# Expert matmuls moved between the attention products, one PSUM tensor for the output, and expert weights loaded by two queues

## The chip, the cores and the metric

The kernel runs on one Trainium2 chip, on 8 cores at once. Every core runs the same program on its own sequence of 4096 tokens; the cores exchange nothing. The metric is the device time in microseconds of the slowest core. Profiled executions show in addition each core's span, from its first to its last instruction.

## The reference

A token's 1024 features are normalised to `xn`. Two branches read `xn`, and the output is `x + attention(xn) + expert(xn)`:

```python
xn = _layernorm(x, axis=-1)
# attention branch: heads of ONE token attend to each other (16 heads x 64)
q = xn @ Wq + bq
kv = (xn @ Wdown + bdown) @ Wup + bup          # 1024 -> 256 -> 2048
k, v = split(kv.reshape(B, T, 16, 128))
q, k = apply_rope(q), apply_rope(k)            # same rotation for all heads
att = softmax(einsum('bthd,btgd->bthg', q, k) / sqrt(64))
a = einsum('bthg,btgd->bthd', att, v).reshape(B, T, 1024) @ Wout + bout
# expert branch: top 1 of 8 experts
logits = xn @ router_w.T + router_b
w, top1 = max(softmax(logits)), argmax(logits)
f = (xn @ expert_w[top1].T + expert_b[top1]) * w
```

Query and key of one token are rotated by the same angle, so the rotation drops out of their product, and the kernel leaves it out.

## The kernel before, in words

**Tiling.** A core works through its 4096 tokens in 16 tiles of 256 (`for i in range(nt)`). Ahead of the loop stands a phase of some 400 us, in which weights are loaded and cast to bf16, and the eight expert matrices (2 MB each in bf16) are transposed and written to a tensor in HBM, `exscratch`. SBUF has room for only two expert matrices, the two halves of `exbuf`, so that in each tile all eight are read again, 16 MB.

**One tile.** TensorE's order within a tile is: transpose `xn` (L666), router (L677), `q` (L685), the routing mask (L693, L701), the latent (L708), keys and values (L720), then for the two halves w = 0 and 1 of the tile the transposes of the values and the query-key products (L730 to L752), then the two products of attention with the values, slots `av0` (L760, into PSUM tensor `psb`) and `av1` (L772, into `psa`), then the output projection `wout` (L787, with the bias row at L792), then the eight experts (L804, 64 matmuls of 128x256 each), the expert bias (L811), and the transposes back to token order `yT` (L818). Output projection and experts add up in the same PSUM: four of the eight 256-column blocks in `psb`, four in `psa`, one to a bank.

**The experts.** Every expert is computed for all 256 tokens; VectorE first multiplies `xn` by a mask row that is zero for tokens of another expert, which gives `xe` (L389 for experts 0 and 1, L442 for the others; two buffers). `xe` of expert n may be written once expert n-2 is done (semaphore `sxu`). The weights follow the same rule: SyncE waits on `sxu` for expert n-2 and then issues one DMA of 2 MB into that half of `exbuf` (L832 is the helper's line).

**The softmax.** For each half w VectorE adds a mask, takes the maximum, subtracts (L398 to L407), ScalarE exponentiates (L573, L584), VectorE sums, divides (L413 to L424) and transposes the result into `pav` (L433). There is one `pav`: the transpose for w = 1 waits until `av0` has read the one for w = 0. ScalarE then copies each half's product from PSUM to `o_f` (slots `of0`, L597, and `of1`, L608). Of the eight `xe` multiplies the last six stand behind the second transpose in VectorE's list.

**What sets the order.** Nothing reorders instructions. Each engine has its own list, written by hand, and the engines wait for each other by counters: TensorE's, ScalarE's and VectorE's steps have numbered slots (`T_SLOTS`, `S_SLOTS`, `V_SLOTS`), and `tensor.wait_ge(smV, vv(i, 'pav0'))` waits until VectorE has passed slot `pav0` of tile i. L197 and L475 in the profile are the helpers that close such a slot on VectorE and ScalarE. GpSimd's list only issues DMAs in the loop: after the last step of a tile (`yadd`) the load of the tokens two tiles ahead, and the two stores of the output (L170).

Of the kernel before, what the change touches and what calls it, by code (L numbers as in the profile page):

```python
# [17 lines left out]
           'vT0', 'qk0', 'vT1', 'qk1', 'av0', 'av1', 'wout', 'expert', 'yT']  # L18
# [5 lines left out]
P0_T = 4 + 64  # L24
P0_S = 65
P0_V = 53
P0_SEX = 16 * 8
# [14 lines left out]
def build_core(dbg_dump=None, nt=NT, phase0_only=False):  # L42
# [22 lines left out]
    with ExitStack() as st:  # L65
# [72 lines left out]
        sex1 = e(nc.semaphore("sex1"))  # L138
        sexp = e(nc.semaphore("sexp"))
# [14 lines left out]
        def _(gpsimd):  # L154
# [24 lines left out]
            if not phase0_only:  # L179
# [3 lines left out]
                for i in range(nt):  # L183
                    gpsimd.wait_ge(smV, vv(i, 'yadd'))
                    if i + 2 < nt:
                        xload(i + 2)
                    for g in range(2):
                        gdma(out_d[TOK * i + 128 * g:TOK * i + 128 * (g + 1), :],
                             outsb[:, 1024 * g:1024 * (g + 1)], so)

        @block.vector
        def _(vector):
# [92 lines left out]
            for i in range(nt):  # L285
# [161 lines left out]
                vector.wait_ge(smT, tv(i, 'expert'))  # L447
                if i > 0:
                    vector.wait_ge(smT, tv(i - 1, 'yT'))
                srcyb = re(psb[:], "p (m x) -> p m x", x=512)[:, :, 0:256]  # L450
                vector.tensor_copy(out=re(y_f[:, 0:1024], "p (m x) -> p m x", x=256),
                                   in_=srcyb)
                srcya = re(psa[:], "p (m x) -> p m x", x=512)[:, :, 0:256]
                vector.tensor_copy(out=re(y_f[:, 1024:2048], "p (m x) -> p m x", x=256),
                                   in_=srcya)
# [14 lines left out]
        def _(scalar):  # L470
# [22 lines left out]
            for i in range(nt):  # L493
# [95 lines left out]
                for hl in range(2):  # L589
                    for a in range(4):  # L590
                        srco = re(psb[64 * hl:64 * hl + 64, :],
# [21 lines left out]
        def _(tensor):  # L613
# [7 lines left out]
            li = None  # L621
# [38 lines left out]
            for i in range(nt):  # L660
# [95 lines left out]
                tinc(li)  # L756
                tensor.wait_ge(smV, vv(i, 'pav0'))
                for ol in range(16):
                    for a in range(4):
                        li = tensor.matmul(  # L760
                            out=psb[:, 512 * a + 32 * ol:512 * a + 32 * (ol + 1)],
# [5 lines left out]
                tinc(li)  # L767
                tensor.wait_ge(smV, vv(i, 'pav1'))
                tensor.wait_ge(smS, sv(i, 'extr1'))
# [11 lines left out]
                tensor.wait_ge(smS, sv(i, 'of0'))  # L781
                tensor.wait_ge(smS, sv(i, 'of1'))
                def pout(m):
                    return (psb if m < 4 else psa)[:, 512 * (m % 4):512 * (m % 4) + 256]
                for m in range(8):
                    for k in range(8):
# [4 lines left out]
                                      start=(k == 0), stop=False)  # L791
                    li = tensor.matmul(out=pout(m),  # L792
                                       lhsT=bo_r[:, 128 * m:128 * (m + 1)],
                                       rhs=ones_b[:], start=False, stop=False)
                tinc(li)
                for ex in range(8):
                    n = 8 * i + ex
                    tensor.wait_ge(sxv, n + 1)
                    tensor.wait_ge(sex0 if n % 2 == 0 else sex1, 16 * (n // 2 + 1))
                    eb = 8192 * (n % 2)  # L800
                    xb = 2048 * (ex % 2)
                    for m in range(8):
                        for k in range(8):
                            li = tensor.matmul(out=pout(m),  # L804
                                               lhsT=exbuf[:, eb + 1024 * k + 128 * m:
                                                           eb + 1024 * k + 128 * (m + 1)],
                                               rhs=xe[:, xb + 256 * k:xb + 256 * (k + 1)],
                                               start=False, stop=False)
                    li.then_inc(sxu, 1)
                for m in range(8):  # L810
                    li = tensor.matmul(out=pout(m),  # L811
                                       lhsT=exb[:, 128 * m:128 * (m + 1)],
# [134 lines left out]
```

## Time and profile before

| | us |
|---|---|
| Time, median of 3 runs (lowest, highest) | 3315.51 (3314.82, 3319.16) |
| The profiled execution's own time | 3312.88 |
| Its span on the slowest core, core 1 | 3311.3 |
| Spans of the eight cores | 3260.0 to 3311.3 |
| TensorE matmuls busy | 1932.0 (58%) |
| VectorE busy | 861.2 (26%) |
| ScalarE busy | 558.2 (17%) |
| GpSimd busy | 35.0 (1%) |

A page of the profile has the busy time of each engine, the span in 40 slices with TensorE's granted clock (1.00 is 2.4 GHz, 0.50 is 1.2 GHz), the DMA queues, the chain of work that ended last, and the costliest groups of instructions with the idle time before them and what ended it. PE is TensorE, PEld its weight loads, DVE VectorE, ACT ScalarE, POOL GpSimd, SP SyncE. An ending q, as in DVEq, is the engine's sequencer, here nearly always a slot being closed. The DMA queues are two: q1, issued by SyncE, moved 330.40 MB, and q0, issued by GpSimd, 33.56 MB. On the chain that ended last TensorE has 47% of the span, DMA 20%, VectorE 14% and ScalarE 8%.

### The profile page before, as it was taken

Reading aid. Unit: us, or ns where it says so; the run is one execution under the profiler, and the core shown is the slowest. Engines: PE = TensorE matmul, PEld = TensorE weight load, DVE = VectorE, ACT = ScalarE, POOL = GpSimd, SP = SyncE. Lnnn points to the kernel's source line nnn. Section 1 sums busy time; section 2 is a strip of 40 time slices with the busy share of each in tenths; the row PEclk is TensorE's granted clock in tenths of the full one; section 3 lists DMA queues with packets and bytes.
Section 4 is the critical chain, followed back from the end, with each engine's and each line's share of the span. In section 5 each row is a group of like instructions: output and inputs, shape, how many; then the busy total and the mean of one; then the engine's idle time right before and its main releaser. Section 6 shows DMA issues by size and latency. Waiting matters only on the chain.

```text
span 3311.3 us, 38330 instructions; the slowest of 8 cores (3260.0 to 3311.3 us)
## 1 busy us (share of the span) xinstructions
PE 1932.0 (58%) x16558; PEld 1572.4 (47%) x16558; DVE 861.2 (26%) x1041; ACT 558.2 (17%) x770; POOL 35.0 (1%) x74
## 2 busy tenths in 40 slices
PE   0011158576675757485766657574858576575758
PEld 0011147455454636374555546363646455463636
DVE  2111131322323232313223232323131322323231
ACT  0122230211112030303011120303030211203030
POOL 0000000000000000000000000000000000000000
PEclk9855569687776869596867768686969677776869
DMA  5344414132240506050322315060504133140504
GB/s 157 135 152 152 168 61 178 52 131 99 80 150 33 197 1 229 1 200 29 136 94 83 147 45 185 1 229 1 209 20 166 64 115 115 56 174 8 209 1 165
DMA packets 42362, 366.40 MB, mean 111 GB/s; under 512 B 5059, under 2 KB 6083, under 8 KB 24532
## 3 DMA queue, kind: packets, MB, share of 16 engines
q1 hardware_dynamic: 32980, 330.40, 27.2%
q0 software_dynamic: 9216, 33.56, 3.2%
q8 instruction: 132, 2.16, 0.3%
q14 instruction: 34, 0.28, 0.0%
HBM read 330.39 MB, written 33.55 MB: 110 GB/s over the span
## 4 chain that ended last, share of the span: by engine, by line
PE 47%; DMA 20%; DVE 14%; ACT 8%; issue 4%; DVEq 4%; ACTq 3%; SPq 1%; POOL 0%; POOLq 0%
DMA exbuf<-exscratch 13%; PE psb L804 9%; PE psa L804 8%; PE psb L720 6%; DMA y_f<-exw 5%; PE psb L685 5%; PE psa L677 3%; PE psb L787 3%; ACTq L475 3%; DVE pav L433 2%; DVE pdiag L424 2%; PE psa L787 2%; ACT koct L544 2%; ACT vdm L549 2%; DVEq L197 2%
## 5 line engine op out<-in xcount | busy, mean ns | idle before, releaser
L804 PE MATMUL psb<-xe,exbuf 128*128 128x256 bf16 x4096 | 485.6, 279 | 94.7 <-DMA exbuf<-exscratch 94.5
L804 PEld LDWEIGHTS psb<-xe,exbuf 128*128 128x128 bf16 x4096 | 402.8, 100 | 168.8 <-issue 113.3
L804 PE MATMUL psa<-xe,exbuf 128*128 128x256 bf16 x4096 | 468.1, 273 | 0.0
L804 PEld LDWEIGHTS psa<-xe,exbuf 128*128 128x128 bf16 x4096 | 400.8, 98 | 46.4
L442 DVE TENSOR_TENSOR xe<-xnf,mrep 128x2048 bf16<-128x2048 bf16 x96 | 117.6, 1225 | 917.9 <-PE psa L804 917.9
L720 PE MATMUL psb<-lat,wup_sb 128*128 128x256 bf16 x1024 | 190.9, 365 | 123.0 <-ACTq L475 123.0
L496 ACT ACTIVATE lnv<-mv,epsc 128x2 f32<-128x2 f32 x16 | 4.8, 300 | 1334.3 <-DVEq L197 1334.3
L720 PEld LDWEIGHTS psb<-lat,wup_sb 128*128 128x128 bf16 x1024 | 125.9, 127 | 188.4 <-issue 147.9
L651 PE MATMUL psa<-idbf,exbuf 128*128 128x128 bf16 x512 | 49.4, 280 | 260.0 <-DVE exbuf L280 256.7
L651 PEld LDWEIGHTS psa<-idbf,exbuf 128*128 128x128 bf16 x512 | 46.0, 131 | 263.3 <-issue 263.1
L677 PE MATMUL psa<-rT_sb,xnf 128*128 128x8 f32 x512 | 111.5, 361 | 79.1 <-DVEq L197 79.1
L685 PE MATMUL psb<-xnf,wq_sb 128*128 128x256 bf16 x1024 | 152.5, 325 | 0.0
L677 PEld LDWEIGHTS psa<-rT_sb,xnf 128*128 128x128 f32 x512 | 110.4, 332 | 83.7 <-issue 83.7
L666 PE MATMUL psb<-id,xn_t 128*128 128x128 f32 x256 | 56.1, 411 | 149.2 <-ACTq L475 149.2
L685 PEld LDWEIGHTS psb<-xnf,wq_sb 128*128 128x128 bf16 x1024 | 121.3, 120 | 30.1
L787 PE MATMUL psb<-o_f,wo_sb 128*128 128x256 bf16 x512 | 104.9, 373 | 43.0 <-ACTq L475 43.0
L666 PEld LDWEIGHTS psb<-id,xn_t 128*128 128x128 f32 x256 | 51.4, 224 | 153.9 <-issue 153.9
L280 DVE CAST exbuf<-y_f 128x2048 bf16<-128x2048 f32 x32 | 39.3, 1227 | 260.1 <-DMA y_f<-exw 260.1
L487 ACT COPY exbuf<-psa 128x1024 bf16<-128x1024 bf16 x64 | 59.4, 1049 | 250.3 <-PE psa L651 250.3
L367 DVE TENSOR_TENSOR qoct<-qoct,qpatb 128x4096 bf16<-128x4096 bf16 x16 | 36.7, 2292 | 238.2 <-ACTq L475 238.2
L526 ACT ACTIVATE qoct<-psb 64x2048 bf16<-64x2048 f32 x32 | 78.0, 2437 | 121.2 <-PE psb L685 121.1
L772 PE MATMUL psa<-pav,vst 32*128 32x32 bf16 x1024 | 11.0, 187 | 148.6 <-DVEq L197 148.6
(128 smaller groups left out, 1806.1 us busy)
## 6 DMA issues: line engine op xcount, KB each, us to landing
exbuf<-exscratch SPq DMA_DIRECT2D x128, 2048.0 KB, 8.4
y_f<-exw SPq DMA_DIRECT2D x64, 512.0 KB
x_t<-x POOLq DMA_DIRECT2D x32, 512.0 KB, 5.7
exscratch<-exbuf SPq DMA_DIRECT2D x8, 2048.0 KB, 7.8
out<-outsb POOLq DMA_DIRECT2D x32, 512.0 KB, 6.9
y_f<-wq SPq DMA_DIRECT2D x8, 512.0 KB
y_f<-wo SPq DMA_DIRECT2D x8, 512.0 KB
y_f<-wup SPq DMA_DIRECT2D x2, 1024.0 KB
```

The costliest lines, as they stand in the source:

```text
L197: ins = vector.drain()
L424: vector.tensor_tensor(out=dstn, in0=srcn, in1=r3.broadcast_to([32, 16, 32]), op=ALU.mult)
L442: vector.tensor_tensor(out=re(xe[:, 2048 * (ex_i % 2):2048 * (ex_i % 2) + 2048], "p (cc t) -> p cc t", t=256), in0=src0, in1=m1.broadcast_ ...
L475: ins = scalar.drain()
L526: scalar.activation(out=dstq, in_=srcq, func=AF.Identity, scale=0.125)
L651: li = tensor.transpose(out=psa_bf[:, 1024 * (kd % 4) + 128 * jo: 1024 * (kd % 4) + 128 * (jo + 1)], in_=exbuf[:, 1024 * jo + 128 * kd:102 ...
L666: li = tensor.transpose(out=psb[:, 128 * (8 * g + cc):128 * (8 * g + cc + 1)], in_=xn_t[:, 1024 * g + 128 * cc:1024 * g + 128 * (cc + 1)], ...
L677: li = tensor.matmul(out=psa[:, off:off + 8], lhsT=xnf32[:, 128 * (8 * g + cc): 128 * (8 * g + cc + 1)], rhs=rT[:, 8 * cc:8 * cc + 8], sta ...
L685: li = tensor.matmul(out=psb[:, 256 * m:256 * (m + 1)], lhsT=wq[:, 1024 * k + 128 * m: 1024 * k + 128 * (m + 1)], rhs=xnf[:, 256 * k:256 * ...
L720: li = tensor.matmul(out=psb[:, 256 * gch:256 * (gch + 1)], lhsT=wup[:, 4096 * k + 128 * ch: 4096 * k + 128 * (ch + 1)], rhs=lat[:, 256 * ...
L787: tensor.matmul(out=pout(m), lhsT=wo[:, 1024 * k + 128 * m: 1024 * k + 128 * (m + 1)], rhs=o_f[:, 256 * k:256 * (k + 1)], start=(k == 0), ...
L804: li = tensor.matmul(out=pout(m), lhsT=exbuf[:, eb + 1024 * k + 128 * m: eb + 1024 * k + 128 * (m + 1)], rhs=xe[:, xb + 256 * k:xb + 256 * ...
```

## The change

The order within a tile changes on TensorE. After the query-key products come four matmuls that write zeros to all of `psb` (a row of `unit` that holds zeros as the one-row left operand), then experts 0 and 1, then `av0`, experts 2 and 3, `av1`, experts 4 to 7, and last, block by block, the expert bias, the output projection and its bias row. `av0` now writes `psa` as `av1` does, so `av0` waits for `extr1` (ScalarE's copy of the second query-key product out of `psa`), and `av1` for `of0` (ScalarE's copy of `av0`). All eight output blocks stand side by side in `psb`, two to a bank, and VectorE copies them to `y_f` in one instruction. The slots `expert` and `wout` change places.

The load of an expert's weights is split by columns: SyncE issues the first 4096 columns, GpSimd the other 4096, each 1 MB, with the same wait on `sxu` and with semaphores of its own (`sexg0`, `sexg1`), for which TensorE waits too.

```diff
 T_SLOTS = ['xnT', 'router', 'q', 'prepA', 'prepB', 'lat', 'kv0', 'kv1', 'kv2', 'kv3',
-           'vT0', 'qk0', 'vT1', 'qk1', 'av0', 'av1', 'wout', 'expert', 'yT']
+           'vT0', 'qk0', 'vT1', 'qk1', 'av0', 'av1', 'expert', 'wout', 'yT']
...
@@ gpsimd
                 for i in range(nt):
+                    for ex in range(8):
+                        n = 8 * i + ex
+                        if n == 0:
+                            gpsimd.wait_ge(smT, P0_T)
+                            gpsimd.wait_ge(sexp, P0_SEX)
+                        if n >= 2:
+                            gpsimd.wait_ge(sxu, n - 1)
+                        gdma(exbuf[:, 8192 * (n % 2) + 4096:8192 * (n % 2) + 8192],
+                             exs_d[ex][:, 4096:8192],
+                             sexg0 if n % 2 == 0 else sexg1)
                     gpsimd.wait_ge(smV, vv(i, 'yadd'))
...
@@ vector
-                vector.wait_ge(smT, tv(i, 'expert'))
+                vector.wait_ge(smT, tv(i, 'wout'))
                 if i > 0:
                     vector.wait_ge(smT, tv(i - 1, 'yT'))
-                srcyb = re(psb[:], "p (m x) -> p m x", x=512)[:, :, 0:256]
-                vector.tensor_copy(out=re(y_f[:, 0:1024], "p (m x) -> p m x", x=256),
-                                   in_=srcyb)
-                srcya = re(psa[:], "p (m x) -> p m x", x=512)[:, :, 0:256]
-                vector.tensor_copy(out=re(y_f[:, 1024:2048], "p (m x) -> p m x", x=256),
-                                   in_=srcya)
+                vector.tensor_copy(out=y_f[:], in_=psb[:])
+                vector.drain()
                 vinc()
...
@@ scalar, slot of0
-                        srco = re(psb[64 * hl:64 * hl + 64, :],
+                        srco = re(psa[64 * hl:64 * hl + 64, :],
...
@@ tensor
+                def pout(m):
+                    return psb[:, 256 * m:256 * (m + 1)]
+
+                def expert_mms(ex):
+                    n = 8 * i + ex
+                    tensor.wait_ge(sxv, n + 1)
+                    tensor.wait_ge(sex0 if n % 2 == 0 else sex1, 16 * (n // 2 + 1))
+                    tensor.wait_ge(sexg0 if n % 2 == 0 else sexg1, 16 * (n // 2 + 1))
+                    eb = 8192 * (n % 2)
+                    xb = 2048 * (ex % 2)
+                    for m in range(8):
+                        for k in range(8):
+                            li = tensor.matmul(out=pout(m), ..., start=False, stop=False)
+                    li.then_inc(sxu, 1)
+                    return li
+
+                tensor.wait_ge(smS, sv(i, 'kv3ev'))
+                for b in range(4):
+                    tensor.matmul(out=psb[:, 512 * b:512 * (b + 1)],
+                                  lhsT=unit[0:1, 128:256], rhs=unit[0:1, 0:512],
+                                  start=True, stop=False)
+                expert_mms(0)
+                expert_mms(1)
                 tensor.wait_ge(smV, vv(i, 'pav0'))
+                tensor.wait_ge(smS, sv(i, 'extr1'))
                 # av0: 64 matmuls
-                            out=psb[:, 512 * a + 32 * ol:512 * a + 32 * (ol + 1)],
+                            out=psa[:, 512 * a + 32 * ol:512 * a + 32 * (ol + 1)],
                 tinc(li)
+                expert_mms(2)
+                expert_mms(3)
                 tensor.wait_ge(smV, vv(i, 'pav1'))
-                tensor.wait_ge(smS, sv(i, 'extr1'))
+                tensor.wait_ge(smS, sv(i, 'of0'))
                 # av1: 64 matmuls
                 tinc(li)
-                tensor.wait_ge(smS, sv(i, 'of0'))
+                for ex in range(4, 8):
+                    expert_mms(ex)
                 tensor.wait_ge(smS, sv(i, 'of1'))
                 # then, for each of 8 blocks m: exb (1 matmul), wo (8), bo_r (1)
...
@@ sync
-                    dma(exbuf[:, 8192 * (n % 2):8192 * (n % 2) + 8192], exs_d[ex],
+                    dma(exbuf[:, 8192 * (n % 2):8192 * (n % 2) + 4096],
+                        exs_d[ex][:, 0:4096],
                         sem=sex0 if n % 2 == 0 else sex1)
```

How the instructions stand on TensorE before, from the second query-key product to the first experts of a tile (`pav` is the transposed softmax, `vst` the values, `o_f` the attention's output, `wo_sb` its projection, `xe` the masked tokens; `smV`, `smS` are VectorE's and ScalarE's slots):

```order
L752 MATMUL psa<-koct,qoct 128x128 x15
L760 MATMUL psb<-pav,vst 128x32 [waits smV]
L760 MATMUL psb<-pav,vst 128x32 x63
L772 MATMUL psa<-pav,vst 128x32 [waits smV,smS]
L772 MATMUL psa<-pav,vst 128x32 x63
L787 MATMUL psb<-o_f,wo_sb 128x256 [waits smS]
```

And the same place of the changed kernel, up to the fourth expert:

```order
L760 MATMUL psa<-koct,qoct 128x128 x15
L787 MATMUL psb<-unit_sb 128x512 [waits smS]
L787 MATMUL psb<-unit_sb 128x512 x3
L777 MATMUL psb<-xe,exbuf 128x256 [waits sxv,sex0,sexg0]
L777 MATMUL psb<-xe,exbuf 128x256 x63
L777 MATMUL psb<-xe,exbuf 128x256 [waits sxv,sex1,sexg1]
L777 MATMUL psb<-xe,exbuf 128x256 x63
L796 MATMUL psa<-pav,vst 128x32 [waits smV,smS]
L796 MATMUL psa<-pav,vst 128x32 x63
L777 MATMUL psb<-xe,exbuf 128x256 [waits sxv,sex0,sexg0]
L777 MATMUL psb<-xe,exbuf 128x256 x63
```

Two experts now stand between the query-key products and `av0` (L796), two between `av0` and `av1`, and the projection has moved behind the eighth expert.

VectorE's list at the end of the softmax and the start of the later `xe` multiplies is the same in both kernels but for line numbers; this is the changed kernel's:

```order
L425 TENSOR_REDUCE s<-pex 128x16 [waits smS]
L429 RECIPROCAL r<-s 128x16
L436 TENSOR_TENSOR pdiag<-pex,r 32x16x32 x4
L445 STREAM_TRANSPOSE pav<-pdiag 128x2048 [waits smT]
L454 TENSOR_TENSOR xe<-xnf,mrep 128x2048 [waits sxu] x6
L462 COPY y_f<-psb 128x2048 [waits smT]
```

Nothing moved here: the transpose L445 waits for `av0` (through `smT`), and the multiply for expert 2 stands behind it.

GpSimd's list of the changed kernel, from the first tile into the second (each `exbuf` row is half an expert):

```order
L172 DMA exbuf<-exscratch 128x4096 [waits smT,sexp]
L172 DMA exbuf<-exscratch 128x4096
L172 DMA exbuf<-exscratch 128x4096 [waits sxu] x6
L172 DMA x_t<-x 128x1024 [waits smV]
L172 DMA x_t<-x 128x1024
L172 DMA out<-outsb 128x1024 x2
L172 DMA exbuf<-exscratch 128x4096 [waits sxu] x8
```

Before, it held only the `x_t` and `out` rows. The eight expert loads of a tile now stand between one tile's stores and the next tile's token loads.

## Rows read from the trace of the kernel before

**Rows 1.** The page's head, and VectorE's first step of each tile.
```profile
span 3311.3 us, 38330 instructions; the slowest of 8 cores (3260.0 to 3311.3 us)
...
L289 DVE BATCH_NORM_STATS2 stats<-x_t x32: 675/684/695, 401.1 to 3129.4; 128x6 f32<-128x512 f32 x32
```

**Rows 2.** Waits of TensorE, whole run: us in total, times, longest.
```profile
PE psa L772 <- DVEq L197: 148.6, 16, 9.6
...
PE psb L804 <- DMA exbuf<-exscratch: 94.5, 72, 3.5
...
PE psb L760 <- DVEq L197: 88.0, 16, 5.5
...
PE psb L787 <- ACTq L475: 43.0, 16, 2.7
```

**Rows 3.** Timeline of TensorE, one tile: start, length, instructions, idle before.
```profile
844.32 1.87 PE L752 MATMUL psa<-koct,qoct 128*128 128x128 bf16 x16 [2.18 <-ACTq L475]
851.69 0.69 PE L760 MATMUL psb<-pav,vst 32*128 32x32 bf16 x64 [5.50 <-DVEq L197]
861.64 0.69 PE L772 MATMUL psa<-pav,vst 32*128 32x32 bf16 x64 [9.26 <-DVEq L197]
865.01 1.86 PE L787 MATMUL psb<-o_f,wo_sb 128*128 128x256 bf16 x8 [2.69 <-ACTq L475]
866.81 0.39 PE L792 MATMUL psb<-ones_b,bo_row 1*128 1x256 bf16 x1
867.13 1.89 PE L787 MATMUL psb<-o_f,wo_sb 128*128 128x256 bf16 x8
...
873.74 1.05 PE L787 MATMUL psa<-o_f,wo_sb 128*128 128x256 bf16 x8
...
874.93 1.05 PE L787 MATMUL psa<-o_f,wo_sb 128*128 128x256 bf16 x8
...
877.31 3.67 PE L804 MATMUL psb<-xe,exbuf 128*128 128x256 bf16 x32
...
893.67 3.65 PE L804 MATMUL psb<-xe,exbuf 128*128 128x256 bf16 x32 [2.21 <-DMA exbuf<-exscratch]
...
939.84 0.59 PE L811 MATMUL psa<-indw_f,exb_sb 8*128 8x256 bf16 x4
943.14 3.50 PE L818 MATMUL psa<-id,y_f 128*128 128x128 f32 x16 [2.71 <-DVEq L197]
```

**Rows 4.** Groups by line, whole run: busy us, mean ns, idle before.
```profile
L804 PE MATMUL psb<-xe,exbuf 128*128 128x256 bf16 x4096 | 485.6, 279 | 94.7 <-DMA exbuf<-exscratch 94.5
...
L804 PE MATMUL psa<-xe,exbuf 128*128 128x256 bf16 x4096 | 468.1, 273 | 0.0
L442 DVE TENSOR_TENSOR xe<-xnf,mrep 128x2048 bf16<-128x2048 bf16 x96 | 117.6, 1225 | 917.9 <-PE psa L804 917.9
```

**Rows 5.** Groups by line within one tile, 775.44 to 956.12 us.
```profile
L433 DVE STREAM_TRANSPOSE pav<-pdiag 128x2048 bf16<-128x2048 bf16 x2 | 4.6, 2311 | 0.5 <-issue 0.5
...
L308 DVE COPY xnf<-psb 128x2048 f32<-128x2048 f32 x1 | 2.3, 2290 | 7.0 <-PE psb L666 7.0
```

**Rows 6.** Stretches: busy by engine, then TensorE's clock, DMA share, GB/s.
```profile
865.00:871.00 6.00, 5.99 (x26) 3.23 (x26) 0.00 (x0) 0.00 (x0) 0.00 (x0) 0.50 0.01 3
872.00:877.00 5.00, 5.00 (x40) 3.28 (x38) 0.00 (x0) 0.00 (x0) 0.00 (x0) 1.00 0.00 0
...
802.50:803.00 0.50, 0.00 (x0) 0.00 (x0) 0.44 (x1) 0.50 (x1) 0.00 (x0) 0.99 0.00 0
803.00:803.50 0.50, 0.00 (x0) 0.00 (x0) 0.50 (x1) 0.49 (x2) 0.00 (x0) 0.50 0.00 0
```

**Rows 7.** Timeline of TensorE: an expert of the first tile, behind a wait.
```profile
563.90 5.32 PE L804 MATMUL psb<-xe,exbuf 128*128 128x256 bf16 x32 [2.30 <-DMA exbuf<-exscratch]
```

**Rows 8.** DMA issues of the whole run: KB each, median us to landing.
```profile
exbuf<-exscratch SPq DMA_DIRECT2D x128, 2048.0 KB, 8.4
...
x_t<-x POOLq DMA_DIRECT2D x32, 512.0 KB, 5.7
```

**Rows 9.** GpSimd's issues after a tile, and the stretches behind them.
```profile
768.87 1.05 POOL L170 DMA_DIRECT2D x_t<-x  x2 [177.86 <-DVEq L197]
...
769.00:770.00 1.00, 0.00 (x0) 0.00 (x0) 1.00 (x3) 0.00 (x0) 1.00 (x3) 0.50 0.00 0
...
771.00:777.00 6.00, 1.56 (x8) 1.59 (x9) 0.44 (x3) 2.87 (x4) 0.00 (x0) 0.50 0.96 326
```

More of the change, by code:

```diff
@@ L138, in build_core @@
         sex1 = e(nc.semaphore("sex1"))
+        sexg0 = e(nc.semaphore("sexg0"))
+        sexg1 = e(nc.semaphore("sexg1"))
         sexp = e(nc.semaphore("sexp"))
@@ L756, in _ @@
                 tinc(li)
+                def pout(m):
[9 more added lines that the diff above has]
+                        for k in range(8):
+                            li = tensor.matmul(out=pout(m),
+                                               lhsT=exbuf[:, eb + 1024 * k + 128 * m:
+                                                           eb + 1024 * k + 128 * (m + 1)],
+                                               rhs=xe[:, xb + 256 * k:xb + 256 * (k + 1)],
+                                               start=False, stop=False)
+                    li.then_inc(sxu, 1)
[7 more added lines that the diff above has]
+                expert_mms(1)
                 tensor.wait_ge(smV, vv(i, 'pav0'))
+                tensor.wait_ge(smS, sv(i, 'extr1'))
                 for ol in range(16):
@@ L780, in _ @@
                 tinc(li)
-                tensor.wait_ge(smS, sv(i, 'of0'))
+                for ex in range(4, 8):
+                    expert_mms(ex)
                 tensor.wait_ge(smS, sv(i, 'of1'))
-                def pout(m):
-                    return (psb if m < 4 else psa)[:, 512 * (m % 4):512 * (m % 4) + 256]
                 for m in range(8):
+                    li = tensor.matmul(out=pout(m),
+                                       lhsT=exb[:, 128 * m:128 * (m + 1)],
+                                       rhs=indw_f[:], start=False, stop=False)
+                    if m == 0:
+                        tinc(li)
                     for k in range(8):
@@ L790, in _ @@
                                       rhs=o_f[:, 256 * k:256 * (k + 1)],
-                                      start=(k == 0), stop=False)
+                                      start=False, stop=False)
                     li = tensor.matmul(out=pout(m),
                                        lhsT=bo_r[:, 128 * m:128 * (m + 1)],
[L794 to L812, printed above, removed]
-                                       rhs=indw_f[:], start=False, stop=True)
+                                       rhs=ones_b[:], start=False,
+                                       stop=(m % 2 == 1))
                 tinc(li)
```

## The prediction, made before the changed kernel had run

> **What bounds the kernel now.** I read first how often the 16 tiles come round: VectorE's first step of a tile stands at 401.1 us in the first and 3129.4 us in the last, (3129.4 - 401.1) / 15 = 181.9 us apart [rows 1]. The loop is 16 x 181.9 = 2910 of the span's 3311.3 us, so a microsecond saved per tile is 16 in all. Then I read TensorE's waits by what ended them [rows 2], since every engine works through a handwritten list and TensorE's is the longest. Four waits lie in the part of the tile that the change rewrites: 88.0 / 16 = 5.5 us ahead of `av0` and 148.6 / 16 = 9.3 us ahead of `av1` (both for VectorE's softmax), 43.0 / 16 = 2.7 us ahead of the output projection (for ScalarE's copy), and 94.5 / 16 = 5.9 us within the experts, for their weights. Last I read one tile's timeline [rows 3]. TensorE stands in a chain there: query-key product until 846.2, `av0` at 851.69, `av1` at 861.64, projection 865.01 to 877.31, experts from there, bias until 940.4. The experts need only `xe` and weights, which for experts 0 and 1 lie ready, yet they queue behind the whole softmax. So TensorE's order bounds this stretch, with work at hand during 17.5 us of waiting.
>
> **What the change does to each wait.** All terms are per tile, against the profiled execution.
>
> *Waits removed.* Experts 0 and 1 now cover the wait for `pav0`. Two experts run from 877.31 to the next wait at 893.67 - 2.21 = 891.46, 7.1 us each [rows 3]; so 14.2 us of work stand where the wait was 5.5. Before `av1` stand experts 2 and 3, another 14.2 us, and behind it four experts cover ScalarE's copy, 28 us against 2.7. Removed: 5.5 + 9.3 + 2.7 = 17.5 us.
>
> *A wait added.* VectorE has one `pav`. Its second transpose waits for `av0`, and the multiply that makes `xe` for expert 2 stands behind that transpose in VectorE's list. Before, this cost nothing extra since TensorE was itself waiting for the transpose. Now `av0` comes only after experts 0 and 1, the softmax of w = 1 has long been done by then, and VectorE is held at the transpose. From the end of `av0`: 0.25 us for the signal, 2.31 for the transpose [rows 5], 0.25 to the next instruction, 1.23 for the multiply [rows 4], 0.15 to TensorE: 4.2 us in which TensorE idles before expert 2. Queued behind the transpose on VectorE are also the multiplies for experts 3 to 7, but each of those is needed 7 us later than the one before and takes 1.23, so only expert 2 waits. Cost: 4.2 us, and I hold this for certain within 0.5.
>
> *The weights' wait.* A load is issued when expert n-2 ends and lands 8.4 us later in the median [rows 8]; expert n-1 covers 7.1 of it. With 0.2 us for the signals every second expert waits 1.5 us (a wait delays the next issue and so pays for the next expert): 3 x 1.5 = 4.5 by this rule, measured 5.9 [rows 2], a factor of 1.3 for the spread. In the new order expert 2 has 7.1 + 0.9 (`av0` with its signals) + 4.2 = 12.2 us for its load, expert 3 has more than 12, since expert 2 follows the 4.2 us gap, and expert 4 has 7.1 + 0.9 (`av1`). Left are 2 x 1.5 - 0.9 = 2.1, times 1.3 = 2.7 us. Saved: 5.9 - 2.7 = 3.2 us, if both halves of a load together still land in 8.4.
>
> *The two halves.* The trace before has no expert load on GpSimd's queue. The nearest rows are its token loads: issued at 768.87, the share of the DMA engines is 0.00 until 770 and 0.96 after 771, at 326 GB/s [rows 9]. So this queue starts at least 1.1 us after its first issue, and then keeps the engines as full as SyncE's does, which needs 8.4 us for 2 MB. Bounds: the two 1 MB halves overlap their fixed costs and land up to 1 us sooner, or GpSimd's half ends up to 3 us later. A microsecond either way moves the wait by 2 us per tile (experts 4 and 6). I take no change, the value nearest to 8.4, since the bytes and the 16 engines are the same. The Trainium skill says much the same in its page DMA: Bandwidth & Descriptors, section Issuing engines are not separate DMA queues: DMAs of several engines end on the same 16 and gain only the time to start them. [...]
>
> *The clock.* Before, the projection starts at 1.2 GHz (0.50 from 865 to 871) and is at 2.4 GHz from 872 [rows 6]; it takes 877.31 - 865.01 = 12.3 us, and at the high clock a block takes 874.93 - 873.74 = 1.19, eight 9.5. At the tile's end, straight behind four experts, it has the high clock. Saved: 2.8 us. Now expert 0 meets the low clock instead. The clock rose between 871 and 872, some 6.5 us after dense work began at 865.01. Dense work now begins with the query-key product at 844.32 or, at the latest, with expert 0 at about 848.1; so between 2.7 and 6.5 us of expert 0 run at half speed, and half of that is lost, 1.3 to 3.2. I take 1.8, nearer to the first, since TensorE has no wait from 844.32 on. The second place is the new 4.2 us gap with `av0`'s 0.7 us ahead of it. In the trace the clock fell to 0.50 at 803, with TensorE idle [rows 6], and even a wait of 2.30 us was followed by a group of 32 matmuls that took 5.32 instead of 3.65 us, 1.7 lost [rows 3, 7]. So I expect the clock to fall in the gap and expert 2 to start at 1.2 GHz. Bounds 1.7 (that row) and 3.2 (half of 6.5), and 0 if the high clock survives the gap. I take 2.4. On the other side such falls cost the experts 485.6 - 468.1 = 17.5 us in the run [rows 4], 1.1 per tile (some ten falls behind the 72 waits of rows 2), of which with fewer and shorter waits I leave 0.4. Net of the clock: 2.8 + 0.7 - 1.8 - 2.4 = -0.7.
>
> *Small terms.* Four zero matmuls of 512 columns: at the low clock a one-row matmul of 256 columns takes 867.13 - 866.81 = 0.32 us, of which about 0.1 is the change of operands; twice the columns give 0.43 each and 1.9 with the start. At the high clock it would be 1.0. The two signals ahead of `av0` and `av1`, where TensorE now arrives with its partner done: 0.4 in all. The expert bias is moved, 8 matmuls as before: 0. VectorE's one copy of 2048 columns: 2.29 by the like copy from PSUM [rows 5], against the 2.7 us between bias and `yT` that the two copies and their signals take now [rows 3]; one instruction less, one drain more, 0 within 0.1. GpSimd's list: its halves for experts 0 and 1 of the next tile stand behind the token loads and stores issued at about 769; tokens, stores and the two halves are 4 MB, at 326 GB/s 13 us from 770 on, and they are needed at 846, 60 us of cover. The token loads themselves wait for the same slot as before, and six expert loads ahead of them are long issued by then.
>
> **The sum** per tile: 17.5 + 3.2 - 4.2 - 0.7 - 1.9 - 0.4 = 13.5 us saved. Times 16: 216. The profiled execution took 3312.9 us; 3312.9 - 216 = 3097. It stands 2.6 us under the median of the runs, so I forecast 3100 us.
>
> **The rivals.**
> *The clock stays up.* The 4.2 us gap doesn't lower it, and it has risen when expert 0 begins: 2.4 + 1.8 = 4.2 us more per tile, 17.7 in all: 3312.9 - 283 + 2.6 = 3032 us. For it: only some ten of 72 waits in the experts lowered it [rows 2, 4]. Against: the fall at 803 [rows 6]. 12%.
>
> *GpSimd's half is late.* GpSimd's queue moves nothing for 1.1 us after an issue [rows 9], and each of its loads now fires at the moment when VectorE starts an `xe` multiply. With 2 us of lag the wait grows by 4 us per tile: 13.5 - 4 = 9.5, 3164 us. For it: the token loads need 5.7 us for 512 KB [rows 8]. Against: those are 2 MB in flight at once. 20%. The Trainium skill, page SBUF — State Buffer, section Who interferes with whom, has a rule against DMAs issued from GpSimd: while VectorE is in a two-port mode, GpSimd can't write its descriptors; it excepts `tensor_tensor`, as this multiply is. No row before shows such a pair.
>
> *Slower than before.* Two DMAs at once, one on each queue, land later than one of the same bytes, by so much that it eats all. A landing time L beyond 8.4 costs 2 (L - 8.4) at experts 4 to 7, and beyond 12.2 another L - 12.2 at expert 2. The 13.5 us are gone at 3 L = 42.5, L = 14.2 us; at L = 15 the cost is 13.2 + 2.8 = 16.0, and the kernel takes 3315.5 + 16 x 2.5 = 3356 us. It would need 1 MB from GpSimd's queue at some 80 GB/s; rows 9 show 326 for the queue. 3%.
>
> *The change doesn't do what it says.* If weights or `xe` of experts 0 and 1 weren't ready at 846, the wait would only move, and the time be 3310 to 3316. The weights have had since the tile before, and both multiplies stand ahead of the softmax in VectorE's list. 2%. Denser work on all cores could also take the clock in the experts under 1.00; a sixth lost on some 66 us of dense matmuls is 11 us, which leaves 13.5 - 11 = 2.5 and 3276 us. 3%.
>
> **How the numbers follow.** Forecast 60%, 3100, own range 3065 to 3140. With clock kept 12% (3032), late half 20% (3164), slower 3%, no effect 2%, denser work 3%. The range of 8 in 10 reaches from the middle between the forecast and the first rival, 3050, to a little past the late half, 3175. A difference of 0.2% (6.6 us) is about what a measurement of this kernel can tell from none. Faster by more: 60 + 12 + 20 + 3 = 95%; within 2%; slower 3%.
>
> **What would show it.** The period of tiles, 168.4 us instead of 181.9. TensorE's waits ahead of `av0`, `av1` and the projection under 0.5 us each. A wait of about 4.2 us in each tile before expert 2, ended by VectorE's `xe` multiply, and behind it a group at 0.50 clock; if it isn't there, I misread VectorE's list. Waits for expert weights of some 2.7 us per tile, at experts 4 and 6; 6 or more would mean the late half, and then the landing of GpSimd's issues must exceed SyncE's. The projection at 9.5 us plus 0.9 for the bias, all at 1.00. Wrong would be the forecast if the waits vanish as said and the experts themselves take more than 7.1 us.

## The result and the profile after

| | before | changed |
|---|---|---|
| Median, us (lowest, highest; 8 runs each) | 3316.88 (3313.21, 3325.39) | 3104.83 (3100.08, 3116.60) |
| Ratio to before (95% interval) | 1 | 0.9365 (0.9351 to 0.9380) |
| Span of the profiled execution, us | 3311.3 | 3099.9 |

The forecast was 3100 us, in a range of 3050 to 3175. The medians are 212 us apart, 216 were forecast. In some executions of a kernel the cores of one die show a lower granted clock and the time is 1 to 3% longer; the times and ratios below are those of the executions without it.

The page's head and VectorE's first step of each tile answer to [rows 1]:

```profile
span 3099.9 us, 38858 instructions; the slowest of 8 cores (3082.9 to 3099.9 us)
...
L301 DVE BATCH_NORM_STATS2 stats<-x_t x32: 675/682/695, 402.2 to 2922.8; 128x6 f32<-128x512 f32 x32
```

The tiles come (2922.8 - 402.2) / 15 = 168.0 us apart, where the prediction had 168.4, and before 181.9. The first starts at 402, before at 401: all of the gain lies in the loop.

TensorE's waits, as in [rows 2] (us in total, times, longest):

```profile
PE psb L777 <- DVE xe L454: 69.1, 16, 4.5
PE psb L777 <- DMA exbuf<-exscratch: 60.3, 46, 3.1
PE psa L842 <- DVEq L209: 43.3, 16, 3.0
```

No row is left for `av0` (now L796), `av1` (L810) or the projection (L829), which before stood at 88.0, 148.6 and 43.0 us. One row is new: 16 waits of 4.3 us for the `xe` multiply L454. The wait for expert weights fell from 94.5 to 60.3 us.

TensorE's timeline of one tile, which answers to [rows 3] (start, length, instructions, idle before):

```profile
816.09 1.86 PE L760 MATMUL psa<-koct,qoct 128*128 128x128 bf16 x16 [2.18 <-ACTq L483]
817.89 1.88 PE L787 MATMUL psb<-unit_sb 1*128 1x512 bf16 x4
819.70 15.51 PE L777 MATMUL psb<-xe,exbuf 128*128 128x256 bf16 x128
835.15 0.65 PE L796 MATMUL psa<-pav,vst 32*128 32x32 bf16 x64
840.11 15.54 PE L777 MATMUL psb<-xe,exbuf 128*128 128x256 bf16 x128 [4.30 <-DVE xe L454]
855.58 0.65 PE L810 MATMUL psa<-pav,vst 32*128 32x32 bf16 x64
856.52 7.15 PE L777 MATMUL psb<-xe,exbuf 128*128 128x256 bf16 x64 [0.28 <-DMA exbuf<-exscratch]
865.07 14.13 PE L777 MATMUL psb<-xe,exbuf 128*128 128x256 bf16 x128 [1.41 <-DMA exbuf<-exscratch]
880.76 7.15 PE L777 MATMUL psb<-xe,exbuf 128*128 128x256 bf16 x64 [1.56 <-DMA exbuf<-exscratch]
...
901.11 3.57 PE L842 MATMUL psa<-id,y_f 128*128 128x128 f32 x16 [2.69 <-DVEq L209]
```

A row of 128 matmuls is two experts. Behind a wait that left the clock up, or none, two take 14.13 us. The first two of the tile take 15.51 and the next two 15.54, 1.4 us more each: that is the low clock. In other tiles the low clock took more: up to 2.9 us from the first two experts (17.07 us from 1485.53 on) and up to 2.2 from the next two. From the zeros to the end of the projection the tile has no other idle time than the 4.30 us and three waits for weights.

VectorE around that wait, which shows why it is 4.3:

```profile
835.97 2.31 DVE L445 STREAM_TRANSPOSE pav<-pdiag 128x2048 bf16<-128x2048 bf16 x1 [5.43 <-PE psa L796]
838.52 2.36 DVE L454 TENSOR_TENSOR xe<-xnf,mrep 128x2048 bf16<-128x2048 bf16 x2 [0.24 <-issue]
```

VectorE had stood idle for 5.43 us until `av0` (L796) was done, then made the transpose, and only then the multiply that TensorE needed (the second row holds two multiplies, for experts 2 and 3). TensorE's clock in the same stretch (length, busy of PE, PEld, DVE, ACT, POOL, then the granted clock, the DMA share and GB/s):

```profile
836.00:838.00 2.00, 0.00 (x0) 0.00 (x0) 2.00 (x1) 1.98 (x7) 0.28 (x1) 1.00 0.64 197
838.00:840.00 2.00, 0.00 (x0) 0.00 (x0) 1.76 (x3) 0.41 (x2) 0.00 (x0) 0.90 1.02 414
840.00:842.00 2.00, 1.89 (x10) 1.33 (x11) 0.88 (x1) 0.00 (x0) 0.00 (x0) 0.50 0.97 410
...
844.00:846.00 2.00, 2.00 (x21) 1.78 (x20) 0.00 (x0) 0.00 (x0) 0.00 (x0) 1.00 0.00 0
```

The clock fell within the idle time, expert 2 began at 0.50 (1.2 GHz), and by 844 it was back at 1.00 (2.4 GHz).

The groups of matmuls over the whole run, against [rows 4], and the DMA issues, against [rows 8]:

```profile
L777 PE MATMUL psb<-xe,exbuf 128*128 128x256 bf16 x8192 | 971.6, 284 | 129.6 <-DVE xe L454 69.1
...
L728 PE MATMUL psb<-lat,wup_sb 128*128 128x256 bf16 x1024 | 186.1, 359 | 123.0 <-ACTq L483 123.0
...
L829 PE MATMUL psb<-o_f,wo_sb 128*128 128x256 bf16 x1024 | 134.0, 274 | 0.0
...
exbuf<-exscratch SPq DMA_DIRECT2D x128, 1024.0 KB, 5.2
exbuf<-exscratch POOLq DMA_DIRECT2D x128, 1024.0 KB, 8.4
```

The projection has the high clock in all tiles (274 ns each). SyncE's half of a load lands after 5.2 us and GpSimd's after 8.4, which is just what the whole load took before.

### The profile page after: what moved, and what is told of

It is laid out like the page before. It is cut to its first block, busy times and chain, and to the rows that moved or that the text cites. A ratio compares the mean times of both kernels' runs of the same rounds, so it can differ in the third digit from the quotient of the medians.

```text
span 3099.9 us, 38858 instructions; the slowest of 8 cores (3082.9 to 3099.9 us)
## 1 busy us (share of the span) xinstructions
PE 1961.9 (63%) x16622; PEld 1580.3 (51%) x16622; DVE 859.0 (28%) x1025; ACT 558.7 (18%) x770; POOL 102.3 (3%) x202
## 4 chain that ended last, share of the span: by engine, by line
PE 56%; DMA 16%; DVE 10%; ACT 8%; issue 4%; DVEq 3%; ACTq 2%; SPq 1%; POOL 0%; POOLq 0%
PE psb L777 24%; DMA exbuf<-exscratch 9%; PE psb L728 6%; DMA y_f<-exw 6%; PE psb L693 5%; PE psb L829 4%; PE psa L685 4%; ACT koct L552 2%; ACT vdm L557 2%; PE psb L674 2%; PE psa L716 2%; ACTq L483 2%; PE psa L842 2%; PE psa L659 1%; DVE exbuf L292 1%
## 5 line engine op out<-in xcount | busy, mean ns | idle before, releaser
L777 PE MATMUL psb<-xe,exbuf 128*128 128x256 bf16 x8192 | 971.6, 284 | 129.6 <-DVE xe L454 69.1
L777 PEld LDWEIGHTS psb<-xe,exbuf 128*128 128x128 bf16 x8192 | 827.6, 102 | 276.5 <-issue 153.1
L728 PE MATMUL psb<-lat,wup_sb 128*128 128x256 bf16 x1024 | 186.1, 359 | 123.0 <-ACTq L483 123.0
L454 DVE TENSOR_TENSOR xe<-xnf,mrep 128x2048 bf16<-128x2048 bf16 x96 | 116.2, 1225 | 463.2 <-PE psb L777 459.5
L728 PEld LDWEIGHTS psb<-lat,wup_sb 128*128 128x128 bf16 x1024 | 123.2, 124 | 186.3 <-issue 148.8
L693 PE MATMUL psb<-xnf,wq_sb 128*128 128x256 bf16 x1024 | 153.4, 327 | 0.0
L674 PE MATMUL psb<-id,xn_t 128*128 128x128 f32 x256 | 57.6, 418 | 148.9 <-ACTq L483 148.9
L462 DVE COPY y_f<-psb 128x2048 f32<-128x2048 f32 x16 | 36.7, 2292 | 406.3 <-PE psb L834 406.3
L172 POOL DMA_DIRECT2D exbuf<-exscratch x128 | 67.6, 529 | 2436.9 <-PE psb L777 2020.1
L693 PEld LDWEIGHTS psb<-xnf,wq_sb 128*128 128x128 bf16 x1024 | 121.8, 120 | 30.5
L829 PE MATMUL psb<-o_f,wo_sb 128*128 128x256 bf16 x1024 | 134.0, 274 | 0.0
L674 PEld LDWEIGHTS psb<-id,xn_t 128*128 128x128 f32 x256 | 52.1, 225 | 153.6 <-issue 153.6
L829 PEld LDWEIGHTS psb<-o_f,wo_sb 128*128 128x128 bf16 x1024 | 89.7, 98 | 34.5 <-issue 23.8
L445 DVE STREAM_TRANSPOSE pav<-pdiag 128x2048 bf16<-128x2048 bf16 x32 | 74.0, 2311 | 98.5 <-PE psa L796 94.8
```

What stands on the lines that cost most here:

```text
L172: gpsimd.dma_start(out=dst, in_=src).then_inc(sem, 16)
L445: vector.transpose(out=pav[:], in_=pdiag[:])
L454: vector.tensor_tensor(out=re(xe[:, 2048 * (ex_i % 2):2048 * (ex_i % 2) + 2048], "p (cc t) -> p cc t", t=256), in0=src0, in1=m1.broadcast_ ...
L674: li = tensor.transpose(out=psb[:, 128 * (8 * g + cc):128 * (8 * g + cc + 1)], in_=xn_t[:, 1024 * g + 128 * cc:1024 * g + 128 * (cc + 1)], ...
L693: li = tensor.matmul(out=psb[:, 256 * m:256 * (m + 1)], lhsT=wq[:, 1024 * k + 128 * m: 1024 * k + 128 * (m + 1)], rhs=xnf[:, 256 * k:256 * ...
L728: li = tensor.matmul(out=psb[:, 256 * gch:256 * (gch + 1)], lhsT=wup[:, 4096 * k + 128 * ch: 4096 * k + 128 * (ch + 1)], rhs=lat[:, 256 * ...
```

## The experiments

Each ran against the kernel before on the same chip; its ratio is to that. The kernel before had medians of 3312.5 to 3316.9 us in these sessions, so a difference of two medians of the table is good to some 5 us.

| run | edit | median, us | ratio (95% interval) |
|---|---|---|---|
| changed kernel | | 3104.8 | 0.9365 (0.9351 to 0.9380) |
| e1 | changed, loads unsplit | 3097.6 | 0.9353 (0.9323 to 0.9383) |
| e2 | before, loads split | 3329.4 | 1.0050 (1.003 to 1.007) |
| e3 | changed, no expert ahead of `av1` | 3283.3 | 0.9916 (0.9889 to 0.9944) |
| e4 | changed, `xe` for expert 2 earlier | 3034.6 | 0.9155 (0.9135 to 0.9175) |
| e5 | changed, half of each load earlier | 3014.1 | 0.9092 (0.9068 to 0.9115) |
| e6 | e4 and e5 | 2933.4 | 0.8868 (0.8832 to 0.8903) |
| e7 | changed, zeros twice | 3133.4 | 0.9457 (0.9433 to 0.9481) |
| e8 | before, loads as two DMAs of SyncE | 3327.9 | 1.0043 (1.0026 to 1.0060) |
| e9 | e6 without zeros | 2879.5 | 0.8713 (0.8681 to 0.8745) |
| e10 | changed, projection between experts 5 and 6 | 3057.1 | 0.9227 (0.9213 to 0.9242) |

### The two parts of the change apart: e1, e2, e8

```diff
 e1, on the changed kernel
-                    for ex in range(8):              # gpsimd: its half of each load
-                        ...
-                    dma(exbuf[:, 8192 * (n % 2):8192 * (n % 2) + 4096],
-                        exs_d[ex][:, 0:4096],
+                    dma(exbuf[:, 8192 * (n % 2):8192 * (n % 2) + 8192], exs_d[ex],
                         sem=sex0 if n % 2 == 0 else sex1)
```

> The changed kernel with the expert loads undone: one DMA of 2 MB from SyncE per expert, nothing on GpSimd for them. The new order of the matmuls stays. Theory (the split is worth nothing, the order is worth all): 3105 us within 8, the waits for expert weights 3.8 us per tile as now, the landing 8.4 us. Rival 1 (the split shortened the waits, from 5.9 to 3.8 us per tile): 2.1 x 16 = 34 us slower than the changed kernel, 3139. Rival 2 (GpSimd's half is late and costs 1 us of landing, 2 us per tile): 3073.

Measured: 3097.6 us, 0.9353 against 0.9365, intervals overlapping. The waits for weights are the same:

```profile
PE psb L766 <- DMA exbuf<-exscratch: 60.8, 48, 3.9
```

and the landing is as before the change:

```profile
exbuf<-exscratch SPq DMA_DIRECT2D x128, 2048.0 KB, 8.6
```

The split is worth nothing in the new order, within the 0.3% that these intervals resolve, and the order is the whole gain. Both rivals (3139 and 3073 us) fall.

> The kernel before with the split of the expert loads alone, one half from SyncE and one from GpSimd. Theory: 3317 us within 8, waits for expert weights 5.9 us per tile. Rival 1 (the split helps): up to 5.9 us per tile less, and if it helps as much as 2.1 per tile, 3283. Rival 2 (GpSimd's half late by 1 us, three waits per tile grow by 2 x 1): 3 x 2 x 16 / 2 = 48 us slower, 3365.

Measured: 3329.4 us, 0.5% slower than before, 14 to 17 us, where 3317 within 8 was expected. The waits grew from 94.5 to 113.1:

```profile
PE psb L817 <- DMA exbuf<-exscratch: 113.1, 68, 3.6
```

with these landings (last number, us):

```profile
exbuf<-exscratch SPq DMA_DIRECT2D x128, 1024.0 KB, 6.0
exbuf<-exscratch POOLq DMA_DIRECT2D x128, 1024.0 KB, 8.8
```

That pointed to GpSimd, whose half lands last. e8 takes GpSimd out and keeps the two halves:

```diff
 e8, on the kernel before
+                    dma(exbuf[:, 8192 * (n % 2):8192 * (n % 2) + 4096],
+                        exs_d[ex][:, 0:4096],
+                        sem=sex0 if n % 2 == 0 else sex1)
+                    dma(exbuf[:, 8192 * (n % 2) + 4096:8192 * (n % 2) + 8192],
+                        exs_d[ex][:, 4096:8192],
+                        sem=sexg0 if n % 2 == 0 else sexg1)
```

> The kernel before with each expert load as two DMAs of 1 MB, both from SyncE. The split between SyncE and GpSimd made that kernel 1.005 times as slow, its waits for weights 113.1 instead of 94.5 us. Theory (GpSimd's later issue and landing, 8.8 us against 6.0 for SyncE's half, costs that): two DMAs from SyncE take 3315 us within 6, ratio 1.000. Rival (two DMAs instead of one cost it, by a second fixed cost or by smaller rows): 3331, ratio 1.005.

Measured: 1.0043, with 112.2 us of waits. My theory fell: the half percent is the cost not of GpSimd but of making a load two DMAs of half the columns. Whether a second fixed cost or the rows of 8 KB instead of 16 KB do it, these runs don't tell, nor why it shows in the old order (113 against 94 us) and not in the new (60.3 against 60.8).

### What filling the waits is worth: e3

```diff
-                expert_mms(0)
-                expert_mms(1)
                 ...                                  # av0
-                expert_mms(2)
-                expert_mms(3)
                 ...                                  # av1
-                for ex in range(4, 8):
+                for ex in range(8):
                     expert_mms(ex)
```

> The changed kernel with all eight experts behind av1, so that nothing stands in the waits for the softmax; zeros, one PSUM tensor, the projection at the end and the split stay. Theory (filling the waits is the gain): against the changed kernel the waits for pav0 and pav1 return, 5.5 - 1.9 (the zeros lie in it) + 9.3, expert weights wait 2.1 us more, and the 4.3 us before expert 2 and its 1.4 us at the low clock go: +9.2 us per tile, 3105 + 147 = 3252. That is still 64 us under the kernel before, for the projection without its wait (2.7) and at the high clock (2.8), less the zeros. Rival (the projection's place and clock are most of the gain): under 3180.

Measured: 3283.3 us, 178 slower than the changed kernel; filling the waits is 178 of the 212 us. The waits are back:

```profile
PE psa L806 <- DVEq L209: 146.6, 16, 9.5
...
PE psb L777 <- DMA exbuf<-exscratch: 99.0, 63, 3.8
...
PE psa L794 <- DVEq L209: 60.9, 16, 3.9
```

I had expected 3252. Against the changed kernel the waits are (146.6 + 60.9 + 99.0 - 60.3 - 69.1) / 16 = 11.1 us per tile more, near the 10.7 of the expectation; but the experts' low clock gave back only (971.6 - 961.3) / 16 = 0.6 instead of 1.4. Against the kernel before it is 32 us or 2.0 per tile faster, where I had 64: I had left out that with the projection at the end expert 0 is the one to start at the low clock: over the 16 tiles of e3 the first two experts took 32.5 us more than 16 times 14.13, 2.0 per tile. The last place of the projection, its lost wait and the zeros in the softmax's shadow are worth those 2.0 us, no more.

### The wait before expert 2: e4

```diff
                     if w == 1:
+                        xe_mul(2)
                         vector.wait_ge(smT, tv(i, 'av0'))
                     ...
                     vector.transpose(out=pav[:], in_=pdiag[:])
-                for ex_i in range(2, 8):
+                for ex_i in range(3, 8):
```

> The changed kernel with VectorE's multiply for expert 2 moved ahead of the second softmax transpose, which waits for av0; it needs only expert 0 to be done. Theory (the 4.3 us before expert 2 are VectorE's order, and the low clock behind them their price): the wait and 1.4 us at the low clock go, 5.7 us per tile; experts 2 and 3 then wait a little for their weights (8.4 us to landing against 7.1 + 0.9), +0.5 to +2 us: 3.7 to 5.2 saved, 3022 to 3046. Rival (the wait only changes its name, since the weights of expert 2 aren't there much sooner than the multiply): under 1 us per tile saved, 3090 to 3105. av1 must not become late: its transpose then runs beside expert 2.

Measured: 3034.6 us, 70 less, within the expected 3022 to 3046. One tile:

```profile
809.85 15.47 PE L780 MATMUL psb<-xe,exbuf 128*128 128x256 bf16 x128
825.25 0.65 PE L799 MATMUL psa<-pav,vst 32*128 32x32 bf16 x64
827.77 14.13 PE L780 MATMUL psb<-xe,exbuf 128*128 128x256 bf16 x128 [1.87 <-DMA exbuf<-exscratch]
```

The 4.3 us are gone, experts 2 and 3 take 14.13 us instead of 15.54, and a part has turned into a wait for weights: 85.3 us in the run against 60.3. Sum: 69.1 + 971.6 - 948.7 - 25.0 = 67 us, where the medians are 70 apart.

### The waits for weights: e5, e6 and e10

```diff
 e5
-                    for m in range(8):
-                        for k in range(8):
+                    for k in range(8):
+                        if k == 4:
+                            li.then_inc(sxh, 1)      # first half of the weights is read
+                            tensor.wait_ge(sexg0 if n % 2 == 0 else sexg1,
+                                           16 * (n // 2 + 1))
+                        for m in range(8):
                             li = tensor.matmul(out=pout(m), ...
 sync
-                        sync.wait_ge(sxu, n - 1)
+                        sync.wait_ge(sxh, n - 1)
```

> The changed kernel with the expert loops turned round: the eight row blocks k outside, the eight output blocks m inside. After k = 3 the first half of the weights is read, and SyncE loads the next expert but one into it 3.5 us sooner; TensorE waits for GpSimd's half only before k = 4. So each half has 3.5 + 7.1 = 10.6 us for 1 MB instead of 7.1. Theory (the waits for weights come from the 7.1 us that cover a landing of 8.4): they fall from 3.8 us per tile to under 0.5, 3.3 x 16 = 53 us and a few at the low clock: 3045. Rival (2 MB per 7.1 us, 295 GB/s, is what the DMA engines and HBM give with all cores loading, so that an earlier start only makes the landing longer): waits stay over 2 us per tile, 3080 to 3105.

Measured: 3014.1 us, 91 less than the changed kernel, where 60 were expected. TensorE's waits have no row for `exbuf` in the loop any more, and the four last experts run without a break:

```profile
845.78 0.65 PE L814 MATMUL psa<-pav,vst 32*128 32x32 bf16 x64
846.48 28.11 PE L781 MATMUL psb<-xe,exbuf 128*128 128x256 bf16 x256
```

So the cover of 7.1 us, not the rate of the DMA queues, made those waits. The two halves now land after 5.7 us (SyncE's) and 5.9 (GpSimd's), where side by side it was 5.2 and 8.4. It gained more than the 60 us of waits: the experts' busy time fell by 971.6 - 956.7 = 14.9 us, and the groups L728 and L693, of which nothing was changed, ran 12 and 6 us shorter (below). That is 93 us, and the two spans lie 3099.9 - 3006.3 = 93.6 apart.

> The early half together with VectorE's multiply for expert 2 moved ahead of the transpose. In that kernel alone the waits for weights are 85.3 us, 5.3 per tile. Theory: both gains add, 3035 - 5 x 16 = 2955, with nothing left between the query-key product and the end of the projection but some clock. Rival (bandwidth): 3000 to 3035.

Measured: 2933.4 us, 171 less than the changed kernel and 22 less than expected. The two gains alone are 70 and 91; together they gave 10 more: e4 by itself had turned 25 us into waits for weights, which the early half then removes, and some 13 went again in the clock, since the five groups that no edit touched (L674, L693, L716, L728 and `yT` in the changed kernel) ran 4 us shorter in e4, 17 in e5 and only 8 in e6. Over the four last experts (their length, PE busy, the clock third from the end):

```profile
831.00:859.00 28.00, 27.86 (x256) 24.98 (x256) 3.17 (x3) 2.42 (x8) 1.50 (x3) 1.00 0.77 262
```

e10 gives the last two loads time in another way, by the place of the projection:

```diff
                 # av1
-                for ex in range(4, 8):
+                for ex in range(4, 6):
                     expert_mms(ex)
                 tensor.wait_ge(smS, sv(i, 'of1'))
                 # expert bias, projection, bias row
+                expert_mms(6)
+                expert_mms(7)
+                # 4 matmuls of 32 columns with zeros close the banks
```

> The changed kernel with the projection and the expert bias between experts 5 and 6 instead of behind expert 7 (four closing matmuls of 32 columns come last). Their 10.4 us give the loads of experts 6 and 7 time. Theory (every second expert waits because its load has 7.1 us of cover): the waits for weights fall from 3.8 to about 2 us per tile, less 0.3 for the closing matmuls: 1.5 x 16 = 24 us faster than the changed kernel, 3081. Rival (the waits follow the rate of the DMA queues and not the cover): 3105 within 6.

Measured: 3057.1 us, 48 less where 24 were expected. The waits fell by 24 us, as expected:

```profile
PE psb L777 <- DMA exbuf<-exscratch: 36.2, 28, 2.6
```

Some 16 us more came again from the clock. Its group for `yT` (busy us, mean ns, idle before):

```profile
L847 PE MATMUL psa<-id,y_f 128*128 128x128 f32 x256 | 42.6, 337 | 43.3 <-DVEq L209 43.3
```

That was 50.2 us in the changed kernel, and the groups L693, L716 and the experts took 3.7, 3.0 and 1.7 us less. That makes 24 + 16 - 4 for the closing matmuls = 36 us, and the two profiled executions lie 3099.9 - 3061.3 = 38.6 us apart; the other 9 us of the 48 are how far the medians stand from these two executions.

### The zeros: e7 and e9

```diff
 e7
-                for b in range(4):
-                    tensor.matmul(..., start=True, stop=False)
+                for bb in range(8):
+                    b = bb % 4
+                    tensor.matmul(..., start=(bb < 4), stop=False)
 e9, on e6
-                for b in range(4): ...
-                               start=False, stop=False)
+                               start=(ex == 0 and k == 0 and m % 2 == 0),
+                               stop=False)
```

> The changed kernel with eight zero matmuls instead of four (the second four add zeros). They stand at the low clock ahead of expert 0 and take 0.45 us each. Theory (they cost their length): +1.8 x 16 = 29 us, 3134. Rival (as dense work they bring the rise of the clock nearer to expert 0, which gives half back): +0.9 x 16 = 14 us, 3119.

Measured: 3133.4 us against 3104.8, 29 us or 1.8 per tile, as the theory had it. The experts behind took no less (975.3 us against 971.6): more zeros ahead of them brought no clock.

> The kernel with both edits (VectorE's multiply for expert 2 ahead of the transpose, and the early half of the loads), and without the four zero matmuls: expert 0's first matmul into each PSUM bank clears it (start=True at k = 0 for even m), the others add. Theory (the zeros cost their length, 1.8 us per tile, as their doubling showed): 2933 - 29 = 2904. Rival (without them the clock rises later within expert 0, which takes half of it back): 2918.

Measured: 2879.5 us, 54 less than e6 where 29 were expected, and the fastest kernel of the study, 0.8713 of the kernel before. The zeros' length explains 29. The rest is the clock, and neither the theory nor the rival had it: without the zeros expert 0 lost less to the low clock, not more. The groups of core 0, whose span was 2876.3 us:

```profile
L784 PE MATMUL psb<-xe,exbuf 128*128 128x256 bf16 x8192 | 913.2, 274 | 0.6
L732 PE MATMUL psb<-lat,wup_sb 128*128 128x256 bf16 x1024 | 194.7, 371 | 123.2 <-ACTq L487 123.2
L697 PE MATMUL psb<-xnf,wq_sb 128*128 128x256 bf16 x1024 | 155.2, 329 | 0.0
...
L846 PE MATMUL psa<-id,y_f 128*128 128x128 f32 x256 | 33.3, 287 | 43.3 <-DVEq L210 43.3
```

In e6, whose profiled core had a span of 2928.6 us, they took 936.0, 181.0, 147.7 and 54.5. So the experts and `yT` got 22.8 and 21.2 us cheaper and the two others 13.7 and 7.5 dearer; with the 30.1 us of the zeros that is 52.9, and the spans are 52.3 apart. The first two experts of a tile show it:

```profile
793.83 14.83 PE L784 MATMUL psb<-xe,exbuf 128*128 128x256 bf16 x128
```

They lost 14.83 - 14.13 = 0.7 us at the low clock, in e6 15.66 - 14.13 = 1.5. Why the clock rises sooner without the zeros, no run here shows.

Core 4, the slowest of this execution (2903.3 us), is no measure of the edit. Cores 4 to 7 went through the experts of two tiles at a granted clock of 0.81, which no core of another profiled execution shows, and its four last experts took 33.77 us there:

```profile
688.99 33.77 PE L784 MATMUL psb<-xe,exbuf 128*128 128x256 bf16 x256
```

## Why the prediction was right, point by point

**Waits removed, 17.5 us per tile.** Right: the three rows are gone, and e3 brings two of them back for 178 us.

**The added wait, 4.2 us.** Right: 69.1 / 16 = 4.3, behind the transpose on VectorE as said. e4 shows that it was the order of VectorE's list and nothing else: with one instruction moved the wait is gone.

**The waits for weights, 5.9 down to 2.7.** The step is right and the term mis-sized: 60.3 / 16 = 3.8. I had counted two waits per tile and let the spread add 30%. There were 46 in 16 tiles, 2.9 per tile, since the 0.9 us of `av1` don't cover a load that lands late (in the tile above all three came after `av1`). e5 confirms the mechanism.

**The two halves.** I took no change; e1 shows none here. GpSimd's half lands 3.2 us behind SyncE's, but at the time of the undivided load. The late half, my rival at 20%, is so in its landing and not in its effect. Nor is it GpSimd's queue that is late: in e5, where SyncE's half starts 3.5 us sooner, GpSimd's lands after 5.9 us instead of 8.4. The Trainium skill's rule (DMA: Bandwidth & Descriptors, Issuing engines are not separate DMA queues) that DMAs of several engines gain only the time to start them agrees with e1. Its other rule, that VectorE in a two-port mode starves GpSimd's descriptors but `tensor_tensor` doesn't (SBUF — State Buffer, Who interferes with whom), meets no contrary row: GpSimd's issues beside `xe` multiplies take 527 to 542 ns, the token loads 527 in the median. The first rule leaves next to nothing to gain, and neither names the cost of two smaller DMAs, which e8 shows.

**The clock, -0.7 us.** The parts were off and cancel. The projection gained (104.9 + 67.0 - 134.0) / 16 = 2.4 us, with its bias row 2.6, of 2.8. For the experts 8 x 16 times 7.05 us, half of 14.13 in the timeline, is 902; of 971.6 some 5 us are restarts (7.15 instead of 7.05 behind each wait), so 65 us or 4.1 per tile were lost at the low clock. I had 1.8 for expert 0, 2.4 for expert 2 and 0.4 left, 4.6. Added up over the 16 tiles, the first two experts took 30.2 us more than at the high clock, 1.9 per tile; the next two 26.5, 1.7 per tile, the lower bound; and the last four 8.1, 0.5. Before it was 1.1: the 926.5 us in which L804 was busy, less 902 and 7 for restarts. Net: 2.6 + 1.1 - 4.1 = -0.4.

**Small terms.** The zeros cost 1.8 of 1.9 (e7). The bias, the copy to `y_f` (2.69 us between projection and `yT`, before 2.71) and GpSimd's list cost nothing, as said. The two signals ahead of `av0` and `av1`, 0.4 in the prediction, cost nothing either: both start as the matmul before them ends (835.15 and 855.58 in the tile above).

**The sum.** 17.5 + (5.9 - 3.8) - 4.3 - 0.4 - 1.8 = 13.1, where 13.5 were forecast. The span fell by 3311.3 - 3099.9 = 211.4 us, 13.2 per tile, so next to nothing is left unplaced. (The 13.9 us by which the tiles came closer at VectorE's first step leave out the last tile, which got only 4.8 us shorter; taken between the first and the last tile's `yT` it is 13.1.) That the forecast came within 5 us is in part luck: the weights' wait was 1.1 us per tile too good, and the clock, the signals and the zeros together 0.8 too bad.

**The rivals.** *The clock stays up* fell by the row at 840, *slower than before* and *no effect* by the result, *denser work* by the projection at 1.00 and 274 ns in all tiles; what it names is real, though, as the 0.81 in e9's execution shows. The range's lower end was misworked: the middle between 3100 and 3032 is 3066, not 3050, and 3104.8 lies within either.

## What to carry to other kernels

Work that depends on nothing belongs into the waits of a chain on the engine that executes both, and what it gains is the wait's length less whatever then waits behind that engine: here one VectorE instruction that had been free stood 4.3 us behind a transpose, and moving it was worth another 70 us. Before two queues are used for one load, its landing is to be compared with the work that covers it: splitting the bytes gained nothing, issuing half of them when half of the buffer was read gained 91 us. Zeros written only to open an accumulation are matmuls like others, 29 us here, and leaving them out gave 25 more by the clock.

## What the runs showed of the hardware that I had not expected

A load of 2 MB as two DMAs of 1 MB is no faster and can be slower: 1.0043 and 1.005 in the old order, whether SyncE alone or SyncE and GpSimd issue them.

Groups of matmuls get cheaper or dearer in places where nothing was changed, by the clock that they meet. L728's 1024 matmuls (L720 before) took 190.9, 186.1, 174.0 and 181.0 us in the kernel before, the changed one, e5 and e6, with the same waits (123 us) around them, and `yT` took 50.2 us in the changed kernel and 42.6 in e10. A tile's `yT` took 1.94 us at a granted clock of 1.00 on core 0 of e9 (from 711.59 us) and 3.65 at 0.50 in e6 (from 715.43). Some 10 to 20 us, up to 0.7% of the time, can so come with an edit elsewhere, without a part in what the edit was meant to do.

There is a third level of the granted clock besides 1.00 and 0.50: 0.81, on cores 4 to 7 in e9's profiled execution (core 4 from 490 to 560 us and from 671 to 722). Four experts without a break took 33.77 us at it, 28.11 at 1.00.
